# Attention rounds on one Trainium2 core: hop transposes first, score products accumulated on top

## Chip, core and metric

The kernel runs on one core of a Trainium2 chip. The metric is the device time of one execution in microseconds (us), as the median of several runs. Times inside an execution come from a hardware profile of one run.

## What is computed

The reference takes `x` and a context, each 32 batches of 512 positions by 512 features, and a 512 by 512 table of indices into 2017 rows of `rpe`. It runs an mLSTM-like cross attention with 8 heads of 64 features and then a small routed feed-forward layer. What matters here is the attention:

```python
qh = layernorm(x) split into heads;  kh, vh = context split into heads
pe = rpe[hops].reshape(S, S, NH, DH)
k_hop = einsum('bhvc,vmhc->bhvm', qh, pe)
qk = einsum('bhsd,bhtd->bhst', qh, kh / sqrt(DH))
C = (qk + k_hop) * D
h = (C / (normalizer + EPS)) @ vh
```

`D` is a causal decay, zero for keys after the query. So each weight is the sum of a score product (`qk`) and a hop product (`k_hop`), times a decay.

## The kernel before

The program has two parts. In the first, up to about 1350 us, GpSimd gathers rows of `rpe`, TensorE turns them and multiplies them with the queries of all batches, and the hop products go to DRAM. The second part, in which the change lies, works through the 32 batches as overlapping rounds: while batch b is in its attention (`ra` in the code), the next one is prepared (`rp`, `rn`) and the one before goes through its feed-forward layer (`rf`, `rg`). Every engine has its own list of steps, written out by hand in `run`, and semaphores tie the lists together.

A batch has 4 head pairs of 3 units: 12 units, in 6 double steps (`for d in range(DOUBLES)`). A unit takes two heads (`e` = 0, 1) and the causal blocks of 128 by 128 positions that `BLOCKS` lists for it: 4, 4 and 2 blocks for the three units of a pair. Two banks of PSUM belong to each unit of a double step, one bank per head. In a double step TensorE does, in this order:

- `scores` for both units (S, L1689): products of 64 features. Head 0 lies on partitions 0 to 63 and head 1 on 64 to 127, so each matmul uses half of the array's rows, and the two heads' matmuls run side by side. This shape reads `64*128` in the profile. S opens the bank (`start=(n == 0)`).
- `hop_scores` for both units (H, L1701): hop products, laid out by query, are transposed with the identity on the whole array (`128*128`) and added to what S left. Its last transpose tells VectorE that the unit is ready.
- other work on the whole array (called X below): transposes of context, queries and results (L1627), the feed-forward layer's products (L1772, L1776, L1753), a small transpose (L1737). Which of it falls into which double step is written out in the loop.
- `weigh` for both units (V, L1724): decayed weights times values, 64 output features per head, the two heads side by side on the array's columns (`128*64`). It waits for VectorE.

Two small pieces stand between V and S: the gate products (L1664, `128*32`) after the V of d = 2, and the gate rows' transposes (L1674, `40*128`) ahead of d = 5.

VectorE multiplies each ready unit by its decay (L1347). SyncE loads the hop products of a pair into `hop_in` with 16 DMAs (L667). It may do so once a unit of the pair before last has told that it is ready, and the first transposes of a pair (`k == 0`) wait until all 16 have landed. An fp32 matmul stands as two instructions in the trace, a transpose as one.

Of the kernel before, what the change touches and what calls it, by code (L numbers as in the profile page):

```python
# [5 lines left out]
P = 128  # L6
# [91 lines left out]
def build(nc, x, ctxt, hops, igate_w, igate_b, fgate_w, fgate_b, rpe, ln_w, ln_b,  # L98
# [35 lines left out]
    UNITS = len(BLOCKS) * (NH // HPT)  # L134
# [15 lines left out]
    with ExitStack() as ctx:  # L150
        def sem(name):
            return ctx.enter_context(nc.semaphore(name))

        psum = ctx.enter_context(nc.psum_tensor("psum", [P, 8 * BANK], F32))
# [4 lines left out]
        def place(n):  # L159

            top[0] += n
            assert top[0] <= ARENA, top[0]
            return arena[:, top[0] - n:top[0]]

        def bank(n, width=BANK):
            return psum[:, n * BANK:n * BANK + width]


        ident = place(P)
# [47 lines left out]
        qT = [place(KT * S).rearrange("p (k s) -> p k s", k=KT) for _ in range(2)]  # L217
        kT = [place(KT * S).rearrange("p (k s) -> p k s", k=KT) for _ in range(2)]
# [78 lines left out]
        def whole_blocks(n):  # L297

            s, c, k = GROUP[n]
            return c + (k == FULL)  # L300
# [49 lines left out]
        def hop_width(n):  # L350
            s, c, k = GROUP[n]
            return P * s + DIAG * (c + 1)
# [31 lines left out]
        def turn_bank(step):  # L384
            return bank(TURN_BANKS[turned_number[step] % len(TURN_BANKS)])
# [46 lines left out]
        pe_a = Stage(sem("pe_a"), pe_a_steps)  # L432
        dve_a = Stage(sem("dve_a"), [("mul", u) for u in units])
# [1107 lines left out]
        def _(pe):  # L1541
# [5 lines left out]
            for n, (srcs, rows_in, cols, dst, scale, split) in enumerate(jobs):  # L1547
# [10 lines left out]
                for i, src in enumerate(srcs):  # L1558
                    last = nc.tensor.transpose(bank(n % 8)[:, i * cols:(i + 1) * cols], src,
                                               ident[0:rows_in, 0:rows_in])  # L1560
# [20 lines left out]
            for n in range(GROUPS):  # L1581
                s, c, k = GROUP[n]
                width = hop_width(n)
                qt = q_turned[n % 2].rearrange("p (k v b) -> p k v b", k=KT, v=VG)
                for o in hop_order(n):
                    if o[0] in ("diag", "pack"):

                        i = o[1] % 2
                        j = o[2] if o[0] == "diag" else whole_blocks(o[1])
# [7 lines left out]
                    if o[0] != "prod":  # L1597
                        copied(bank_before(o))
                        for q in range(KT):
                            last = nc.tensor.transpose(turn_bank(o)[:, q * P:(q + 1) * P],  # L1600
                                                       own[:, q * P:(q + 1) * P], ident)
                    else:
# [9 lines left out]
                        for p in range(KT):  # L1612
                            for e in range(HPT):
                                at = (3 + 2 * (v % 2) + e) * BANK
                                half = slice(e * DH, (e + 1) * DH)
                                last = nc.tensor.matmul(  # L1616
                                    psum[p * B:(p + 1) * B, at:at + width],
                                    qt[half, p, v, :], rowsT[c % 2][half, v, p, 0:width], start=True, stop=True)
# [5 lines left out]
            def run(rn, rp, ra, rf, rg):  # L1624
# [5 lines left out]
                def turn_context(t):  # L1630

                    if t == 0:
                        pe.wait_ge(ctx_loaded, rp.b * 16 + 16)
                        if rf:
                            pe.wait_ge(dve_o.sem, dve_o.done(rf.b, ("sum", 2)))
                    elif t == 1:
                        if rg:
                            pe.wait_ge(*act_f.at(rg.b, ("mixT", ST - 1)))
                    elif t == 2:
                        if rf:  # L1640
                            pe.wait_ge(dve_o.sem, dve_o.done(rf.b, ("sum", 3)))
                    else:
                        pe.wait_ge(act_p.sem, act_p.done(rp.b, ("c", 1)))
                    turn(C_BANK[t], context[:, t, :]).then_inc(pe_p.sem, pe_p.step(("c", t)))
# [23 lines left out]
                def gate_stats():  # L1668
                    pe.wait_ge(dve_p.sem, dve_p.done(rp.b, "a"))
                    pe.wait_ge(act_p.sem, act_p.done(rp.b, "floor"))  # L1670
                    if rf:
                        pe.wait_ge(*dve_f.at(rf.b, ("out", 1)))
                    for k in range(KT):
                        last = nc.tensor.transpose(bank(6)[:, k * P:k * P + GR], g_rows[0:GR, k * P:(k + 1) * P],  # L1674
                                                   ident[0:GR, 0:GR])
                    last.then_inc(pe_p.sem, pe_p.step("stats"))

                def scores(u):


                    p, k = u // 3, u % 3
                    pe.wait_ge(dve_a.sem, dve_a.done(ra.b, ("mul", (u - 2) % UNITS), 1 if u < 2 else 0))
                    if u == 0:
                        pe.wait_ge(act_p.sem, act_p.done(ra.b, ("x", ST - 1)))
                    at = [((u % 2) * 2 + e) * BANK for e in range(HPT)]
                    for n, (j, col, width) in enumerate(RUNS[k]):
                        for e in range(HPT):
                            half = slice(e * DH, (e + 1) * DH)
                            nc.tensor.matmul(psum[:, at[e] + col:at[e] + col + width],  # L1689
                                             kT[ra.par][half, p, j * P:(j + 1) * P],  # L1690
                                             qT[ra.par][half, p, j * P:j * P + width],
                                             start=(n == 0), stop=False, skip_group_check=True)

                def hop_scores(u):
                    p, k = u // 3, u % 3
                    at = [((u % 2) * 2 + e) * BANK for e in range(HPT)]
                    if k == 0:
                        pe.wait_ge(hop_loaded[p % 2], (ra.b * 2 + p // 2 + 1) * (16 * ST * QUARTERS))
                    for n, (j, i) in enumerate(BLOCKS[k]):
                        for e in range(HPT):  # L1700
                            last = nc.tensor.matmul(psum[:, at[e] + n * P:at[e] + (n + 1) * P],  # L1701
                                                    hop_in[p % 2][:, e, Q_OFF[i] + j * P:Q_OFF[i] + (j + 1) * P],
                                                    ident, is_transpose=True, start=False, stop=True,
                                                    skip_group_check=True)
                    last.then_inc(pe_a.sem, pe_a.step(("score", u)))

                def weigh(u):

# [22 lines left out]
                def turn_back(r, p):  # L1731
                    pe.wait_ge(act_o.sem, act_o.done(r.b, ("turned", p)))
                    turn(pair_bank(p), attT).then_inc(pe_o.sem, pe_o.step(("back", p)))
# [16 lines left out]
                def routes(r, t):  # L1750
                    pe.wait_ge(*act_f.at(r.b, ("xT", t)))
                    for k in range(KT):
                        last = nc.tensor.matmul(bank(7)[:, 0:ER + E_ALL], ffn_xT[t % 2][:, k, :],  # L1753
                                                route_wT[:, k, :], start=(k == 0), stop=(k == KT - 1))
                    last.then_inc(*pe_f.inc(("route", t)))
# [22 lines left out]
                for d in range(DOUBLES):  # L1778
                    if rp and d == 5:
                        gate_stats()  # L1780
                    if ra:
                        scores(2 * d)
                        scores(2 * d + 1)
                        hop_scores(2 * d)
                        hop_scores(2 * d + 1)
                    if d == 0:
                        if rf:
                            turn_back(rf, 3)
                        if rp:
                            turn_context(0)  # L1790
                        if rg:
                            base(rg, 3)
                        elif rp:
                            turn_context(1)
                    if rp and d == 1:
                        turn_context(3)
                        turn_context(2)
                        turn_queries(0)
                        turn_queries(1)
                    if rp and d == 2:  # L1800
                        turn_queries(2)
                    if rf and d == 2:
                        turn_ffn(rf, 0)
                    if ra and d in BACK:
                        turn_back(ra, BACK[d])
                    if rp and d == 2:
                        turn_queries(3)
                    if rf and d >= 3:
                        base(rf, d - 3)
                    if rf and d >= 2:  # L1810
                        routes(rf, d - 2)
                    if ra:
                        weigh(2 * d)
                        weigh(2 * d + 1)
                    if rp and d == 2:
                        gates()

            batch_loop(pe, run)


# [25 lines left out]
```

## Time and profile before

| | us |
|---|---|
| median of 3 runs | 3316.13 |
| lowest and highest run | 3313.09, 3317.16 |
| the profiled execution | 3310.51 |
| its span, first to last instruction | 3308.5 |
| TensorE matmul busy in the span | 2938.0 |
| VectorE busy | 2417.6 |
| GpSimd busy | 2023.2 |
| ScalarE busy | 1941.4 |

The profile's engine names are PE (TensorE matmuls), PEld (TensorE weight loads), DVE (VectorE), ACT (ScalarE), POOL (GpSimd), and SP or SPq (SyncE and its DMA queue). The whole span mixes the two parts of the program, so a share of the span says little about the rounds; the rows below come from stretches within them.

### The profile page before, as it was taken

To read this page: it belongs to the slowest core of one execution; us is meant where nothing else is said; L and a number is where in the kernel's file an instruction comes from. 1 tells how busy PE (TensorE), PEld (TensorE's weight loads), DVE (VectorE), ACT (ScalarE), POOL (GpSimd) and SP (SyncE) were. 2 spreads that over 40 slices of the span, in tenths; PEclk is the share of its full clock that TensorE was granted. 3 is DMA by queue.
4 is the path that set the end of the run, shared out by engine and by line. 5 is a ranking of instruction groups with operands and counts; after the bars stand their busy time and mean duration, and the time that the engine had idled before them with its cause. 6 is when DMAs were issued, how large, how long until landed. Compare 5 with 4: busy or idle time off the path is not lost.

```text
span 3308.5 us, 69970 instructions
## 1 busy us (share of the span) xinstructions
PE 2938.0 (89%) x24660; PEld 1856.5 (56%) x24660; DVE 2417.6 (73%) x5103; ACT 1941.4 (59%) x4654; POOL 2023.2 (61%) x2195
## 2 busy tenths in 40 slices
PE   6777777777777777699999999999999999999998
PEld 4555454544544554366666666666666666666664
DVE  5655555555555555588888888888888888888875
ACT  3444444444444444477666676666766767667663
POOL 6777777777777777256455455564554645546554
PEclk8888899999999999799999999999999999999999
DMA  9999999999999999556556565565565655656542
GB/s 283 345 349 349 320 348 344 344 352 352 347 345 346 351 348 326 190 184 189 180 174 185 178 189 179 177 187 181 177 190 169 195 173 179 187 179 180 185 148 66
DMA packets 414909, 799.98 MB, mean 242 GB/s; under 512 B 107338, under 2 KB 213834, under 8 KB 412516
## 3 DMA queue, kind: packets, MB, share of 16 engines
q1 hardware_dynamic: 312516, 453.08, 43.6%
q0 software_dynamic: 82560, 270.60, 24.5%
q10 hardware_dynamic: 19488, 71.84, 5.6%
q8 instruction: 200, 3.28, 0.4%
q14 instruction: 145, 1.19, 0.1%
HBM read 618.02 MB, written 176.69 MB: 240 GB/s over the span
## 4 chain that ended last, share of the span: by engine, by line
PE 65%; DMA 16%; POOL 9%; issue 5%; DVE 4%; ACT 1%; SPq 0%; POOLq 0%; DVEq 0%; ACTq 0%
DMA arena<-in_L_xattn_rpe_dram,arena 15%; PE psum L1772 13%; PE psum L1689 9%; PE psum L1701 9%; PE psum L1724 9%; PE psum L1627 7%; PE psum L1600 6%; POOL arena L797 6%; PE psum L1616 4%; PE psum L1753 3%; PE psum L1776 3%; PE psum L1664 2%; POOL arena L782 2%; PE psum L1569 1%; DVE arena L1237 1%
## 5 line engine op out<-in xcount | busy, mean ns | idle before, releaser
L797 POOL DMA_INDIRECT arena<-in_L_xattn_rpe_dram,arena x768 | 731.8, 953 | 235.0 <-issue 181.6
L1600 PE MATMUL psum<-arena 128*128 128x128 f32 x4128 | 614.4, 297 | 190.3 <-DMA arena<-in_L_xattn_rpe_dram,arena 178.6
L1600 PEld LDWEIGHTS psum<-arena 128*128 128x128 f32 x4128 | 488.9, 151 | 422.9 <-DMA arena<-in_L_xattn_rpe_dram,arena 292.9
L993 ACT ACTIVATE arena<-arena 128x512 f32<-128x512 f32 (+3 forms) x1024 | 496.3, 555 | 43.7 <-PE psum L1724 39.2
L1772 PE MATMUL psum<-arena 128*128 128x512 f32 x1024 | 493.3, 595 | 0.0
L1347 DVE TENSOR_TENSOR arena<-psum,arena 128x1024 f32<-128x1024 f32 (+1 forms) x384 | 386.6, 1041 | 133.3 <-PE psum L1701 122.4
L573 DVE COPY arena<-psum 128x512 f32<-128x512 f32 x384 | 263.4, 689 | 239.3 <-PE psum L1600 235.5
L582 DVE COPY arena<-psum 128x416 f32<-128x416 f32 (+15 forms) x512 | 225.3, 442 | 278.4 <-PE psum L1616 270.1
L823 POOL TENSOR_SCALAR_AFFINE_SELECT arena<-arena 128x256 f32<-128x256 f32 x256 | 118.7, 464 | 503.9 <-ACT arena L993 491.6
L1616 PE MATMUL psum<-arena 64*32 64x416 f32 (+7 forms) x8192 | 361.5, 422 | 59.3 <-ACT arena L909 38.1
L573 ACT COPY arena<-psum 128x512 f32<-128x512 f32 x384 | 225.8, 588 | 251.7 <-PE psum L1600 248.7
L582 ACT COPY arena<-psum 128x416 f32<-128x416 f32 (+15 forms) x512 | 199.7, 390 | 262.9 <-PE psum L1616 255.5
L1689 PE MATMUL psum<-arena 64*128 64x512 f32 (+3 forms) x2048 | 333.1, 450 | 0.0
L1724 PE MATMUL psum<-arena 128*64 128x512 f32 (+3 forms) x2048 | 318.9, 442 | 5.1 <-ACT arena L965 2.6
L1701 PE MATMUL psum<-arena 128*128 128x128 f32 x2560 | 321.8, 277 | 0.0
L1701 PEld LDWEIGHTS psum<-arena 128*128 128x128 f32 x2560 | 276.2, 140 | 77.5 <-issue 69.9
L782 POOL DMA_INDIRECT arena<-in_L_xattn_rpe_dram,arena x264 | 250.9, 950 | 93.1 <-issue 61.8
L1627 PE MATMUL psum<-arena 128*128 128x128 f32 x2048 | 281.4, 276 | 24.2 <-DMA arena<-in_ctx_dram 11.5
L1627 PEld LDWEIGHTS psum<-arena 128*128 128x128 f32 x2048 | 237.5, 141 | 101.7 <-ACT arena L1044 39.6
L1689 PEld LDWEIGHTS psum<-arena 64*128 64x128 f32 x2048 | 181.3, 187 | 136.9 <-issue 106.5
L1772 PEld LDWEIGHTS psum<-arena 128*128 128x128 f32 x1024 | 168.1, 192 | 113.4 <-issue 113.2
L841 POOL TENSOR_TENSOR arena<-arena 128x512 f32<-128x512 f32 x128 | 159.1, 1243 | 104.4 <-ACT arena L1021 104.4
(112 smaller groups left out, 4632.1 us busy)
## 6 DMA issues: line engine op xcount, KB each, us to landing
arena<-in_x_dram SPq DMA_DIRECT2D x256, 256.0 KB, 4.1
arena<-gate_rows SPq DMA_DIRECT2D x128, 512.0 KB, 4.4
arena<-in_x_dram SPq DMA_DIRECT2D x512, 64.0 KB
arena<-in_ctx_dram SPq DMA_DIRECT2D x32, 1024.0 KB, 7.5
out_dram<-arena SPq DMA_DIRECT2D x128, 256.0 KB, 2.9
arena<-in_L_xattn_rpe_dram,arena POOLq DMA_INDIRECT x1032, 7.1
arena<-hop_products SPq DMA_DIRECT2D x128, 128.0 KB, 2.6
arena<-hop_products SPq DMA_DIRECT2D x128, 120.0 KB, 2.5
```

Source lines behind the costliest of these rows:

```text
L573: copy(rowsT[c % 2][:, o[2], :, o[3] * P:(o[3] + 1) * P], turn_bank(o).rearrange("p (k m) -> p k m", k=KT)).then_inc(*line.inc(o))
L582: copy(hop_out[out_of(n)][:, lo:lo + width], bank(3 + 2 * (v % 2) + i, width)).then_inc(*line.inc(o))
L797: nc.gpsimd.indirect_dma_start(out=rows[set_of(n, v)][:, t, :], out_offset=None, in_=rpe[:, :], in_offset=bass.IndirectOffsetOnAxis(ap=her ...
L993: last = nc.scalar.activation(decay[u % DECAYS][:, e, at:at + width], top_pair[p % 2][:, e * S + j * P:e * S + j * P + width], ACT.Exp, bi ...
L1347: nc.vector.tensor_tensor(d, got[:, :, 0:width], d, ALU.mult).then_inc(dve_a.sem, dve_a.step(("mul", u)))
L1600: last = nc.tensor.transpose(turn_bank(o)[:, q * P:(q + 1) * P], own[:, q * P:(q + 1) * P], ident)
L1616: last = nc.tensor.matmul(psum[p * B:(p + 1) * B, at:at + width], qt[half, p, v, :], rowsT[c % 2][half, v, p, 0:width], start=True, stop=True)
L1627: last = nc.tensor.transpose(bank(b)[:, k * P:(k + 1) * P], src[:, k * P:(k + 1) * P], ident)
L1689: nc.tensor.matmul(psum[:, at[e] + col:at[e] + col + width], kT[ra.par][half, p, j * P:(j + 1) * P], qT[ra.par][half, p, j * P:j * P + width],
L1701: last = nc.tensor.matmul(psum[:, at[e] + n * P:at[e] + (n + 1) * P], hop_in[p % 2][:, e, Q_OFF[i] + j * P:Q_OFF[i] + (j + 1) * P], ident, ...
L1724: last = nc.tensor.matmul(psum[e * DH:(e + 1) * DH, pair_bank(p) * BANK + j * P:pair_bank(p) * BANK + j * P + width], values[ra.par][:, j, ...
L1772: nc.tensor.matmul(bank(6), ffn_xT[t % 2][:, k, :], base_wT[:, k, :], start=(k == 0), stop=False)
```

## The change

Within each double step the calls of `hop_scores` come ahead of those of `scores`. The transposes now open the bank (`start=(n == 0)`), the score products are added to them (`start=False`), and the last score product, not the last transpose, tells VectorE that the unit is ready. The wait for VectorE to have emptied the unit's banks moves to `hop_scores`.

```diff
 def scores(u):
     p, k = u // 3, u % 3
-    pe.wait_ge(dve_a.sem, dve_a.done(ra.b, ("mul", (u - 2) % UNITS), 1 if u < 2 else 0))
     if u == 0:
         pe.wait_ge(act_p.sem, act_p.done(ra.b, ("x", ST - 1)))
...
-                nc.tensor.matmul(psum[:, at[e] + col:at[e] + col + width],
-                                 kT[ra.par][half, p, j * P:(j + 1) * P],
-                                 qT[ra.par][half, p, j * P:j * P + width],
-                                 start=(n == 0), stop=False, skip_group_check=True)
+                last = nc.tensor.matmul(psum[:, at[e] + col:at[e] + col + width],
+                                        kT[ra.par][half, p, j * P:(j + 1) * P],
+                                        qT[ra.par][half, p, j * P:j * P + width],
+                                        start=False, stop=True, skip_group_check=True)
+    last.then_inc(pe_a.sem, pe_a.step(("score", u)))

 def hop_scores(u):
...
+    pe.wait_ge(dve_a.sem, dve_a.done(ra.b, ("mul", (u - 2) % UNITS), 1 if u < 2 else 0))
     if k == 0:
         pe.wait_ge(hop_loaded[p % 2], (ra.b * 2 + p // 2 + 1) * (16 * ST * QUARTERS))
...
-                                    ident, is_transpose=True, start=False, stop=True,
+                                    ident, is_transpose=True, start=(n == 0), stop=False,
                                     skip_group_check=True)
-    last.then_inc(pe_a.sem, pe_a.step(("score", u)))
...
         if ra:
+            hop_scores(2 * d)
+            hop_scores(2 * d + 1)
             scores(2 * d)
             scores(2 * d + 1)
-            hop_scores(2 * d)
-            hop_scores(2 * d + 1)
```

In the changed kernel S is L1688 and H is L1702. Only TensorE's list differs. The double step d = 1 of a batch in mid-loop on TensorE, before (the last row is the V that follows):

```order
L1689 MATMUL psum<-arena 128x256 x2
L1689 MATMUL psum<-arena 128x512 x2
L1701 MATMUL psum<-arena 128x128 x12
L1627 MATMUL psum<-arena 128x128 x16
L1724 MATMUL psum<-arena 64x256 x2
```

The same step in the changed kernel, from the V of the step before:

```order
L1724 MATMUL psum<-arena 64x128 x2
L1702 MATMUL psum<-arena 128x128 x12
L1688 MATMUL psum<-arena 128x256 x2
L1688 MATMUL psum<-arena 128x512 x2
L1627 MATMUL psum<-arena 128x128 x16
L1724 MATMUL psum<-arena 64x256 x2
```

H and X stood side by side before, both on the whole array; now S, on half rows, stands between them. The double step d = 5, before, with the gate rows' transposes L1674 ahead of it:

```order
L1724 MATMUL psum<-arena 64x512 x2
L1674 MATMUL psum<-arena 128x40 x4
L1689 MATMUL psum<-arena 128x384 x2
L1689 MATMUL psum<-arena 128x128 x2
L1689 MATMUL psum<-arena 128x256 x2
L1701 MATMUL psum<-arena 128x128 x12
L1627 MATMUL psum<-arena 128x128 x4
```

And in the changed kernel:

```order
L1724 MATMUL psum<-arena 64x512 x2
L1674 MATMUL psum<-arena 128x40 x4
L1702 MATMUL psum<-arena 128x128 x12
L1688 MATMUL psum<-arena 128x384 x2
L1688 MATMUL psum<-arena 128x128 x2
L1688 MATMUL psum<-arena 128x256 x2
L1627 MATMUL psum<-arena 128x128 x4
```

Here S no longer follows the gate rows' transposes: H stands between them.

## Rows read from the trace of the kernel before

**Rows 1.** Busy time by stretch: the rounds in mid-loop, and one batch.
```profile
core 0: us, PE busy (x) PEld busy (x) DVE busy (x) ACT busy (x) POOL busy (x), PEclk, DMA share, GB/s
1480.00:3200.00 1720.00, 1717.46 (x10569) 1069.28 (x10568) 1496.26 (x3185) 1188.71 (x2898) 935.50 (x1038) 1.00 0.58 180
2004.72:2064.60 59.88, 59.85 (x370) 37.25 (x369) 52.25 (x112) 41.46 (x102) 32.50 (x36) 1.00 0.59 181
```

**Rows 2.** Same view, a stretch in which the first batches enter the rounds.
```profile
1364.84:1424.72 59.88, 49.82 (x364) 32.26 (x364) 41.34 (x67) 41.57 (x93) 17.70 (x31) 0.99 0.64 195
```

**Rows 3.** Chain that ended last, one batch: start us, us, what, pieces end to end.
```profile
2004.79 1.45 PE psum L1724 x12
2006.24 1.93 PE psum L1689 x12
2008.16 1.90 PE psum L1701 x16
2010.06 0.87 PE psum L1627 x8
...
2014.92 0.86 PE psum L1776 x2
2015.78 1.88 PE psum L1724 x12
2017.65 1.49 PE psum L1689 x8
2019.14 1.46 PE psum L1701 x12
2020.60 1.85 PE psum L1627 x16
2022.45 1.44 PE psum L1724 x8
2023.89 1.50 PE psum L1689 x12
2025.39 1.46 PE psum L1701 x12
...
2033.13 1.93 PE psum L1689 x12
...
2046.55 1.46 PE psum L1701 x12
2048.01 1.72 PE psum L1772 x4
...
2055.24 0.31 PE psum L1674 x3
2055.55 1.44 PE psum L1689 x12
2056.98 1.46 PE psum L1701 x12
2058.44 0.44 PE psum L1627 x4
...
2064.67 1.45 PE psum L1724 x12
```

**Rows 4.** Groups by line and shape, 1500 to 3100 us: weight loads, mean ns second.
```profile
L1701 PEld LDWEIGHTS psum<-arena 128*128 128x128 f32 x2132 | 229.9, 140 | 64.9 <-issue 58.5
L1689 PEld LDWEIGHTS psum<-arena 64*128 64x128 f32 x1704 | 149.8, 186 | 112.6 <-issue 87.6
L1772 PEld LDWEIGHTS psum<-arena 128*128 128x128 f32 x858 | 140.0, 191 | 95.0 <-issue 95.0
```

**Rows 5.** Instructions in order of time, d = 1: TensorE and VectorE.
```profile
2017.58 0.73 PEld L1689 LDWEIGHTS psum<-arena 64*128 64x128 f32 x8 [0.17 <-issue]
2017.58 1.56 PE L1689 MATMUL psum<-arena 64*128 64x256 f32 x8
...
2019.77 0.69 DVE L1347 TENSOR_TENSOR arena<-psum,arena 128x512 f32<-128x512 f32 x1 [1.73 <-PE psum L1701]
...
2020.33 1.88 PEld L1627 LDWEIGHTS psum<-arena 128*128 128x128 f32 x16
2020.44 2.01 PE L1627 MATMUL psum<-arena 128*128 128x128 f32 x16
```

**Rows 6.** The same view for SyncE's queue: the loads of hop products, pairs 1 and 2.
```profile
2005.30 8.54 SPq L667 DMA_DIRECT2D arena<-hop_products  x16
...
2019.76 8.62 SPq L667 DMA_DIRECT2D arena<-hop_products  x16
```

**Rows 7.** Line L667, 1500 to 3100 us: issue to landing.
```profile
DMA to landing us min/median/max: 1.5/2.1/4.3
```

## Prediction

> **What bounds the kernel now.** I first read the busy time by stretch. In the rounds TensorE's matmuls cover 1717.46 of 1720 us, with the granted clock at 1.00, which is the 2.4 GHz level, while VectorE has 1496.26 [rows 1]. One batch in mid-loop shows 59.85 of 59.88 us; from one V of d = 5 at 2004.79 to the next at 2064.67 [rows 3] it is 59.88 us too. A busy share alone could hide waits, so I then read the chain that ended last over one batch: it consists of TensorE pieces that follow each other without a gap [rows 3]. In the rounds, therefore, time is what TensorE's own list takes, and the pieces of that list are the thing to cost. The first part of the program, before about 1350 us, is not touched.
>
> **What a piece costs beyond its columns.** In the chain the reader should compare each piece with what its matmuls would take in a steady stream. Eight transposes that follow others of the same layout take 0.87 us, so one takes 0.109 us; a matmul of 512 columns takes 0.43 us (L1776, two in 0.86) [rows 3]. Against that:
>
> - H after S: 16 transposes are 1.74 us and took 1.90; 12 are 1.31 and took 1.46. Entering costs 0.155 us.
> - S after V: of the 12 instructions at 2006.24 six pairs run side by side, 2048 columns, 1.72 us; they took 1.93. The 8 at 2017.65 are 1536 columns, 1.29 us, and took 1.49. Entering costs 0.20 to 0.21 us.
> - V after X: 1536 columns, 1.29 us, took 1.45 and 1.44; 2048 columns, 1.72, took 1.88. Entering costs 0.16 us.
> - X after H: the 8 transposes at 2010.06 are the steady stream itself, so entering costs nothing; H and X have one layout, the whole array [rows 3].
>
> So TensorE pays 0.15 to 0.21 us each time the layout changes (whole array, half rows, half columns), and nothing otherwise. It is not the semaphore waits: H in d = 2 has no wait for hop data, H in d = 1 has one, and both took 1.46 us [rows 3]. It is not the adding onto a filled bank either: V opens its bank in d = 0 and adds in d = 1, and pays 0.16 and 0.15 us.
>
> **The change, part by part.** No matmul, weight load or transpose is added, and the other engines' lists stay. What changes is the number of layout changes. Before, a double step runs V | S | H and X | V: three entries. After, it runs V | H | S | X | V: four, since S now separates H from X.
>
> - Ordinary steps (d = 0 to 3; X begins with transposes): out go S after V (0.21) and H after S (0.155), in come H after V, S after H and X after S. No row shows H after V or S after H. The known entries lie between 0.15 and 0.21 us, and the cost follows what is entered: I take 0.155 for whole-array transposes and 0.21 for S, because these rows are those of the same arriving instructions. X after S arrives with the same kind of transpose as H does: 0.155. Net 0.155 + 0.21 + 0.155 - 0.21 - 0.155 = +0.155 us. In d = 3 the gate products stand between V and S, and the exchange is the same.
> - d = 4: X begins with L1772, whose weight load takes 191 ns, like that of S (186) and unlike that of a transpose (140) [rows 4]. So its entry is put at 0.21 and the step at +0.21 us.
> - d = 5: the gate rows' transposes L1674 use 40 rows, and S after them took 1.44 us for 1.29, an entry of 0.15 [rows 3]. Now H (0.155), S (0.21) and X (0.155) are entered, where S (0.15) and H (0.155) were: +0.21 us.
>
> Per batch 4 x 0.155 + 0.21 + 0.21 = 1.04 us; times 32, 33.3 us. In the stretch where the first batches enter, TensorE is busy for only 49.82 of 59.88 us [rows 2], so there, and likewise at the end, part of it fits into waits; I count 30.5 batches: **+31.7 us**. Against the profiled execution's 3310.5 us this gives 3342; its time stands 5.6 us below the median of 3316.13, so the forecast on the median is **3348 us**.
>
> The bounds: with every new entry at the cheapest one seen (0.15), the steps give 4 x 0.09 + 0.09 + 0.15 = 0.60 us, 18 us in all, 3334. With every new entry at the dearest (0.21), they give 5 x 0.265 + 0.325 = 1.65 us, 50 us in all, 3366.
>
> What rests on cover: VectorE's start. The first unit of d = 1 was handed over 2.19 us after the step began (2017.58 to 2019.77) [rows 5]: S 1.49, H's entry 0.155, four transposes 0.44. Now it is H 1.46, S's entry 0.21, 256 columns in two passes 0.43: 2.10. The second unit is ready at the end of H and S in either order. So VectorE gets its data at about the same distance from V, and X, the cover of its multiplication, even ends 0.155 us later. I cost this at nothing. The moved wait on VectorE is past already: the V ahead of it waited for the same multiplications. The freeing of `hop_in` shifts as little, since it hangs on the same signal.
>
> **A rule beside the rows.** When S begins at 2017.58, its first weight load begins at 2017.58 too, after 0.17 us of idle time, whereas the load for X at 2020.33 runs ahead of its matmul at 2020.44 [rows 5]. The Trainium skill (TensorE: Matmul & The Clock Gate, Part 2, on loading the stationary operand) says that TensorE pulls weight loads ahead of running matmuls. If that held across layout changes too, an entry would shrink by the length of the load and this change would cost some 0.02 us a step, about 3320 us as an estimate; the rows agree with it within a layout and not across one, so I go by the rows. Another page, TensorEngine Tiling (Array Packing), Key Properties, says that changing the tiling mode drains the engine, and lists 128x128, 128x64 and 64x128 as modes of their own: that covers H after V as well, which no row here shows, and speaks against this change.
>
> **Rivals.**
>
> - *Leaving V is free* (3324 us). If whole-array transposes after half columns cost no entry, an ordinary step stays as it was (0.21 + 0.155 either way), d = 4 gains 0.055 and d = 5 keeps 0.21: 0.265 x 30.5 = 8 us more. For it: no row shows this entry. Against it: the opposite change, X to V, costs 0.16 [rows 3].
> - *Faster: the 0.155 at H is a wait for S's results in the bank* (3289 us). Then H, which now opens the bank, has nothing to wait for, and X after S pays nothing either. An ordinary step and d = 4 would lose 0.155 us, d = 5 0.095: 0.87 x 30.5 = 26.5 us less. It decides if H after V and X after S cost under half of 0.155. Against it: V pays the same whether it opens or adds, and S, which opened its banks, paid most.
> - *Hop data come late* (about 3380 us). H now needs its data earlier: pair 1 some 0.6 us into d = 1 instead of 2.1, pair 2 at the start of d = 3. The issues for pair 1 end at 2013.84; with the median landing time of 2.1 us the data are there at 2015.9, with the longest of 4.3 at 2018.1, and H of that pair is due at 2018.2 [rows 5 to 7]. Pair 2's issues end at 2028.38, so its data arrive between 2030.5 and 2032.7, and S of d = 3 began at 2033.13 [rows 3, 6, 7]. So there are 2.3 and 2.6 us to spare at the median and next to nothing at the longest. If landings came 3.3 us later than the median, one such wait of 1 us per batch would add 32 us. Against it: the step begins later too, by what the entries add.
>
> **How the numbers follow.** Forecast 0.83, hop data late 0.08, leaving V free 0.05, faster 0.04. The range 3334 to 3366 takes in the bounds of the entries; outside it lie the rivals, 0.17. A measurement of this kernel can tell about 0.2% from no change, 6.6 us, so 3309.5 to 3322.7 counts as the same. The rival at 3324 lies on that line; I give 0.03 of it to the same and 0.02 to slower. Slower is then 0.83 + 0.08 + 0.02 = 0.93, same 0.03, faster 0.04.
>
> **What would show it right or wrong.** Right: a batch in mid-loop takes about 60.9 us instead of 59.88, TensorE stays busy throughout at a granted clock of 1.00, H at L1702 still takes 1.90 and 1.46 us, S at L1688 1.93 and 1.49, and the first piece of X after S takes 0.15 us more than its columns (8 transposes of d = 0: 1.03 us instead of 0.87). Wrong: H after V without the 0.155, X after S at 0.87 us, or idle time of TensorE ahead of L1702 ended by the hop loads.

## The result, and the profile after

| | us |
|---|---|
| forecast (range) | 3348 (3334 to 3366) |
| median of 3 runs after | 3342.20 (3341.34 to 3347.30) |
| median of 3 runs before | 3316.13 |
| the profiled execution after | 3341.34 |
| its span, first to last instruction | 3339.3 |

The changed kernel is slower: the ratio to the kernel before is 1.0086, with a 95% interval of 1.0073 to 1.0100, and the medians differ by 26.1 us. The two profiled spans differ by 30.8 us. Time in the rounds is still what TensorE's list takes. Busy time of the changed kernel in mid-loop (columns as in [rows 1]):

```profile
1480.00:3200.00 1720.00, 1718.09 (x10414) 1047.68 (x10416) 1461.16 (x3128) 1172.39 (x2856) 907.88 (x1019) 1.00 0.58 178
```

1718.09 of 1720 us are covered by matmuls and the granted clock is 1.00, as in [rows 1]; in the same stretch of time TensorE got through 10414 matmul instructions instead of 10569. So it is not idle more, it needs longer. Where the time went can be read piece by piece in the chain that ended last (start us, us, what), from V of d = 4 of one batch to V of d = 5 of the next:

```profile
2003.16 1.44 PE psum L1724 x8
2004.60 0.37 PE psum L1674 x4
2004.97 1.46 PE psum L1702 x12
2006.43 1.50 PE psum L1688 x12
2007.93 0.58 PE psum L1627 x4
...
2014.31 1.45 PE psum L1724 x12
2015.76 1.90 PE psum L1702 x16
2017.65 1.93 PE psum L1688 x12
2019.58 1.02 PE psum L1627 x8
...
2027.32 1.46 PE psum L1702 x12
2028.78 1.49 PE psum L1688 x8
2030.28 2.00 PE psum L1627 x16
...
2056.59 1.49 PE psum L1688 x8
2058.09 1.92 PE psum L1772 x4
...
2075.22 1.45 PE psum L1724 x12
```

The reader should hold these against [rows 3]. H (now L1702) takes 1.90 and 1.46 us, as before, although it now follows V. S (now L1688) takes 1.93 and 1.49, as before, although it now follows H. What grew is the first piece of X, which now follows S: 8 transposes 1.02 instead of 0.87, 16 transposes 2.00 instead of 1.85, the first feed-forward products 1.92 instead of 1.72, 4 transposes 0.58 instead of 0.44. From one V of d = 5 to the next it is 75.22 - 14.31 = 60.91 us, against 59.88 before: 1.03 us more per batch.

The boundaries themselves, in order of time, in d = 1 of the changed kernel:

```profile
2027.25 1.29 PEld L1702 LDWEIGHTS psum<-arena 128*128 128x128 f32 x12 [0.17 <-issue]
2027.25 1.53 PE L1702 MATMUL psum<-arena 128*128 128x128 f32 x12
2028.71 0.73 PEld L1688 LDWEIGHTS psum<-arena 64*128 64x128 f32 x8 [0.17 <-issue]
2028.71 1.56 PE L1688 MATMUL psum<-arena 64*128 64x256 f32 x8
2029.46 0.69 DVE L1347 TENSOR_TENSOR arena<-psum,arena 128x512 f32<-128x512 f32 x1 [1.75 <-PE psum L1688]
2030.20 0.42 PEld L1627 LDWEIGHTS psum<-arena 128*128 128x128 f32 x4 [0.76 <-issue]
2030.21 0.55 PE L1627 MATMUL psum<-arena 128*128 128x128 f32 x3
```

At each of the three new boundaries the first weight load starts with its stretch and not ahead of it, after idle time of the loader (`[0.17 <-issue]`, `[0.76 <-issue]`): for X at 2030.20 too, whose loads ran 0.11 us ahead of the matmuls in [rows 5], where X followed H. VectorE starts 2.21 us after the step began (2027.25 to 2029.46), against 2.19 before.

### The profile page after: what moved, and what is told of

The parts are those of the page before. It is cut to its first block, busy times and chain, and to the rows that moved or that the text cites. A ratio compares the mean times of both kernels' runs of the same rounds, so it can differ in the third digit from the quotient of the medians.

```text
span 3339.3 us, 70066 instructions
## 1 busy us (share of the span) xinstructions
PE 2979.8 (89%) x24660; PEld 1858.7 (56%) x24660; DVE 2408.2 (72%) x5103; ACT 1942.2 (58%) x4654; POOL 2011.5 (60%) x2195
## 4 chain that ended last, share of the span: by engine, by line
PE 69%; DMA 15%; POOL 7%; issue 4%; DVE 3%; ACT 1%; SPq 1%; DVEq 0%; POOLq 0%; ACTq 0%
DMA arena<-in_L_xattn_rpe_dram,arena 14%; PE psum L1772 13%; PE psum L1688 9%; PE psum L1702 9%; PE psum L1724 9%; PE psum L1600 7%; PE psum L1627 7%; POOL arena L797 6%; PE psum L1616 4%; PE psum L1753 4%; PE psum L1776 3%; PE psum L1664 2%; POOL arena L782 1%; PE psum L1569 1%; DVE arena L1237 1%
## 5 line engine op out<-in xcount | busy, mean ns | idle before, releaser
L1600 PE MATMUL psum<-arena 128*128 128x128 f32 x4128 | 623.4, 300 | 180.8 <-DMA arena<-in_L_xattn_rpe_dram,arena 167.1
L1772 PE MATMUL psum<-arena 128*128 128x512 f32 x1024 | 495.4, 597 | 0.0
L1688 PE MATMUL psum<-arena 64*128 64x512 f32 (+3 forms) x2048 | 328.7, 449 | 0.0
L1702 PE MATMUL psum<-arena 128*128 128x128 f32 x2560 | 324.2, 278 | 1.7 <-DMA arena<-hop_products 1.7
L1702 PEld LDWEIGHTS psum<-arena 128*128 128x128 f32 x2560 | 278.4, 141 | 79.5 <-issue 78.0
L1627 PE MATMUL psum<-arena 128*128 128x128 f32 x2048 | 289.6, 280 | 23.4 <-DMA arena<-in_ctx_dram 11.4
L1772 PEld LDWEIGHTS psum<-arena 128*128 128x128 f32 x1024 | 167.6, 191 | 136.6 <-issue 129.6
L1688 PEld LDWEIGHTS psum<-arena 64*128 64x128 f32 x2048 | 171.1, 186 | 99.1 <-issue 63.0
```

Source lines behind the costliest of these rows:

```text
L1627: last = nc.tensor.transpose(bank(b)[:, k * P:(k + 1) * P], src[:, k * P:(k + 1) * P], ident)
L1688: last = nc.tensor.matmul(psum[:, at[e] + col:at[e] + col + width], kT[ra.par][half, p, j * P:(j + 1) * P], qT[ra.par][half, p, j * P:j * ...
L1772: nc.tensor.matmul(bank(6), ffn_xT[t % 2][:, k, :], base_wT[:, k, :], start=(k == 0), stop=False)
```

## Experiments

The theory: each entry into another layout costs TensorE 0.15 to 0.21 us, by what is entered, and the change adds one entry per double step. The rivals that could give the same slowdown: that H first or S last costs something by itself, or that H meets its data too early. Times of a batch below are the distance of the same V in two successive batches. The edits are shown shortened: the calls of a double step stand on one line, and lines that only follow from what is shown are left out.

**More entries, H still after S.** The units interleaved in the order of before:

```diff
-scores(2 * d); scores(2 * d + 1); hop_scores(2 * d); hop_scores(2 * d + 1)
+scores(2 * d); hop_scores(2 * d); scores(2 * d + 1); hop_scores(2 * d + 1)
```

> The kernel before with the two units' calls interleaved: S of the first unit, H of the first, S of the second, H of the second, then X. Nothing is added but two changes of layout per double step (S after H, H after S). Theory (each entry into another layout costs what the entered instructions cost, 0.155 us for transposes and 0.20 to 0.21 for S): +0.36 us per double step, 6 x 0.36 = 2.2 us per batch, a batch of 62.05 us, and with 30 batches some +65 us, near 3381. Rival (the cost lies in H coming first and S last, not in the number of entries): H still follows S and X still follows H here, so no change, near 3316. Rival (H waits for S's results in the bank): here H follows S of its own unit at once, so each H would wait longest, with H pieces beyond 0.155 us over their stream.

Measured: 3372.19 us against 3314.18, a ratio of 1.0176 (1.0156 to 1.0195), 58 us more. Chain that ended last in this kernel, the pieces of a d = 4 step and, first and last, V of d = 1 in two batches:

```profile
2041.82 1.44 PE psum L1724 x8
...
2065.07 0.63 PE psum L1689 x4
2065.71 0.59 PE psum L1701 x4
2066.30 1.06 PE psum L1689 x4
2067.35 1.02 PE psum L1701 x8
2068.38 1.72 PE psum L1772 x4
...
2103.75 1.44 PE psum L1724 x8
```

S takes 0.63 us for 512 columns (0.43) and 1.06 for 1024 (0.86): 0.20 at each entry. H takes 0.59 for 4 transposes (0.44) and 1.02 for 8 (0.87): 0.15. X after H, which begins with L1772, pays nothing (1.72). A batch takes 61.93 us, 2.05 more where 2.17 was expected. So order is not what costs: H follows S and X follows H here as in the kernel before. H right behind S of its own unit pays no more than elsewhere.

**Six entries.** The changed kernel, interleaved:

```diff
-hop_scores(2 * d); hop_scores(2 * d + 1); scores(2 * d); scores(2 * d + 1)
+hop_scores(2 * d); scores(2 * d); hop_scores(2 * d + 1); scores(2 * d + 1)
```

> The changed kernel with the two units interleaved: H of the first unit, S of the first, H of the second, S of the second, then X. Six entries per double step where the kernel before has three and the changed one four. Theory: H after V 0.16, S after H 0.20, H after S 0.16, S after H 0.20, X after S 0.16, against S after V 0.21 and H after S 0.16: +0.51 us in d = 0 to 3, some +0.56 in d = 4 and 5, 3.2 us per batch, a batch of 63.06 us, some +95 us, near 3411. Rival (only the place of H and S against V and X counts): as the changed kernel, a batch of 60.91 us, near 3342.

Measured: 3403.97 us, a ratio of 1.0271 (1.0252 to 1.0291), 90 us more. V of d = 0 in two batches, from the chain:

```profile
2046.37 1.87 PE psum L1724 x12
...
2109.38 1.88 PE psum L1724 x12
```

63.01 us per batch, 3.13 more than before; 3.2 was expected. With three, four, five and six entries per double step a batch takes 59.88, 60.91, 61.93 and 63.01 us: each entry adds 1.02 to 1.08 us per batch, 0.17 to 0.18 us per double step.

**Four entries, X after H.**

```diff
-scores(2 * d); scores(2 * d + 1); hop_scores(2 * d); hop_scores(2 * d + 1)
+hop_scores(2 * d, True); scores(2 * d, False); scores(2 * d + 1, True); hop_scores(2 * d + 1, False)
```

The second argument says who opens the unit's banks: in the first unit H, in the second S.

> H of the first unit opens its banks, S of both units follows, H of the second unit comes last and adds, then X. Four entries per double step, as in the changed kernel, but X follows H as before, H adds in one unit as before, and the second unit's hop data are needed as late as before. Theory: entries 0.16 + 0.20 + 0.16 against 0.21 + 0.16, +0.155 us per double step, 0.21 in d = 5: a batch of 60.87 us (0.04 less than in the changed kernel, whose d = 4 pays 0.20 for entering the feed-forward products after S), some +29 us, near 3345. Rival (the cost of the change is that X no longer follows H): back to the kernel before, near 3316. Rival (hop data needed earlier): most of the cost gone, since units 3 and 9 need theirs as late as before.

Measured: 3338.86 us, a ratio of 1.0074 (1.0055 to 1.0093), 24.7 us more. In this kernel V is L1730, S L1690, H L1706; chain that ended last, d = 0, and V of d = 3 in two batches:

```profile
2053.03 1.88 PE psum L1730 x12
...
2076.39 1.02 PE psum L1706 x8
2077.41 1.93 PE psum L1690 x12
2079.34 1.02 PE psum L1706 x8
2080.36 0.87 PE psum L1627 x8
...
2113.88 1.87 PE psum L1730 x12
```

X is back at 0.87 us behind H, and the 0.15 that it lost stands in the second H instead (1.02 for 0.87). A batch takes 60.85 us, 0.06 less than in the changed kernel; 60.87 was expected. Neither the place of X nor the time at which hop data are needed explains the cost; the number of entries does.

**The changed kernel again**, beside these three:

> The changed kernel once more, beside the others on one chip: 3342, between 3336 and 3350, a batch of 60.91 us.

Measured: 3344.24 us (3338.31 to 3349.42) against 3314.18, a ratio of 1.0094 (1.0073 to 1.0114).

**The hop data, needed early.** Only the wait is moved, from `hop_scores` to ahead of the double step's S:

```diff
-if k == 0:
-    pe.wait_ge(hop_loaded[p % 2], (ra.b * 2 + p // 2 + 1) * (16 * ST * QUARTERS))
...
+for u in (2 * d, 2 * d + 1):
+    p = u // 3
+    if u % 3 == 0:
+        pe.wait_ge(hop_loaded[p % 2], (ra.b * 2 + p // 2 + 1) * (16 * ST * QUARTERS))
 scores(2 * d)
```

> The kernel before with one thing moved: TensorE waits for the pair's hop data ahead of S of the double step, not ahead of H. This is the earlier need for data that the change brings, without its new entries. Theory (the data have landed by then): no change, 3316 within 0.2%, a batch of 59.88 us, no idle time of TensorE ended by the loads. Rival (hop data come late): each batch waits at d = 1 or d = 3, every 1 us of it 32 us in the run, and the changed kernel's +26 us would be this.

Measured: 3315.17 us against 3313.98, a ratio of 1.0007 (0.9998 to 1.0016): no change that can be told. Waits of its matmuls in the rounds (1360 to 3300 us) on the hop loads, and, second, those of the changed kernel: us in total, times, longest:

```profile
PE psum L1689 <- DMA arena<-hop_products: 1.8, 3, 1.1
...
PE psum L1702 <- DMA arena<-hop_products: 1.7, 1, 1.7
```

Three waits in 32 batches, 1.8 us in all, and one of 1.7 us in the changed kernel.

The data are there in nearly every batch.

**Who opens the bank.** The kernel before, with one flag changed in `hop_scores`:

```diff
-    ident, is_transpose=True, start=False, stop=True,
+    ident, is_transpose=True, start=(n == 0), stop=True,
```

> The kernel before with the transposes opening the banks anew instead of adding: order, waits, shapes and columns as before. What it leaves out: the score products, which the transposes overwrite. Theory (the entry cost belongs to the layout, not to adding): no change, 3316 within 0.2%, H at 1.90 and 1.46 us. Rival (the 0.155 us at H is a wait for S's results in the bank): 0.155 x 6 x 30 = 28 us less, near 3288, H at 1.74 and 1.31 us.

Measured: 3314.74 us against 3313.98, a ratio of 0.9999 (0.9990 to 1.0008). From its chain, H of d = 0 and of d = 1:

```profile
2069.35 1.90 PE psum L1701 x16
...
2080.33 1.46 PE psum L1701 x12
```

The same 1.90 and 1.46 us as with adding. The entry cost does not belong to adding onto S. H still follows S into the same bank here, so this run alone does not rule out a wait for S; the changed kernel does, where H follows V into banks emptied before and takes the same time.

**Fewer entries.** If an entry is the price, taking some away should give time back. V of d = 0 needs nothing that would keep it from running together with V of d = 1:

```diff
-DECAYS = 4
+DECAYS = 6
+WEIGHED = {1: (0, 1, 2, 3), 2: (4, 5), 4: (6, 7, 8, 9), 5: (10, 11)}
...
-weigh(2 * d)
-weigh(2 * d + 1)
+for u in WEIGHED.get(d, ()):
+    weigh(u)
```

> The kernel before with V of d = 0 done together with V of d = 1, and V of d = 3 with V of d = 4 (6 decay buffers instead of 4, so that no decay waits for it). Nothing is added or left out; two entries per batch are gone: X is then followed by S, which is entered at 0.20 where it was 0.21 after V, and V after X (0.15) is saved twice. Theory: 0.3 us less per batch, a batch of 59.58 us, with 30 batches 9 us less, near 3306, 0.997 of before. Rival (the cost of the change is its order, not its entries): the order of S and H is that of before, so no gain, 1.000. Rival (TensorE is not alone on the path): VectorE's multiplications or the decays show as idle time of TensorE ahead of S in d = 1 and 4, and the gain is eaten.

> The same joining of V in the changed kernel. There X of d = 0 and d = 3 is then followed by H, which has the same layout and needs no entry: V after X (0.15) and H after V (0.16) are both saved, twice per batch. Theory: 0.62 us less per batch than the changed kernel, a batch of 60.29 us, some 18 us less than the changed kernel, near 3325, 1.003 of before. Rival (H first costs by itself): only V after X is saved, 0.3 us per batch, near 3334, 1.006 of before.

Measured: 3330.86 us for the first, a ratio of 1.0052 (1.0040 to 1.0065) to the kernel before, and 3352.77 for the second, 1.0111 (1.0094 to 1.0127). Both are slower than the kernels they were made from: a miss. Waits of the first in 1500 to 3100 us, the longest line of TensorE's matmuls:

```profile
PE psum L1665 <- DVE arena L1355: 23.2, 26, 0.9
```

and, in order of time, one of them:

```profile
2097.84 1.27 POOL L847 TENSOR_TENSOR arena<-arena 128x512 f32<-128x512 f32 x1
2097.91 1.23 DVE L1303 TENSOR_SCALAR arena<-arena 128x8 f32<-128x8 f32 x1
...
2098.69 0.61 ACT L1015 ACTIVATE arena<-psum 128x504 f32<-128x504 f32 x1
...
2100.19 0.67 DVE L1355 TENSOR_REDUCE arena<-psum 128x8 f32<-128x504 f32 x1
...
2101.01 1.92 PE L1665 MATMUL psum<-arena 128*32 128x512 f32 x16 [0.89 <-DVE arena L1355]
```

The gate products behind d = 2 (L1665 here) wait for VectorE's sums of pair 0 (L1355), and TensorE stands for 0.89 us in every batch. A batch takes 60.47 us, from 2061.25 to 2121.72 in its chain, and 60.47 - 0.89 = 59.58 is what the theory gave for it without this wait. The second kernel waits there too (`PE psum L1665 <- DVE arena L1355: 19.4, 27, 0.7`), and a batch takes 61.08 us where 60.29 was expected. In the kernel before, this spot was covered by a hair. In order of time there:

```profile
2028.18 1.27 POOL L836 TENSOR_TENSOR arena<-arena 128x512 f32<-128x512 f32 x1
...
2028.91 0.57 DVE L1302 TENSOR_SCALAR arena<-arena 128x8 f32<-128x8 f32 x1
...
2029.72 0.61 ACT L1014 ACTIVATE arena<-psum 128x504 f32<-128x504 f32 x1
...
2030.39 0.67 DVE L1354 TENSOR_REDUCE arena<-psum 128x8 f32<-128x504 f32 x1
...
2031.21 1.93 PE L1664 MATMUL psum<-arena 128*32 128x512 f32 x16
```

VectorE's sums ended at 2031.06, 0.15 us before the gate products began.

The expectation of the next run holds that the sums were late because the V of d = 1 now comes behind the V of d = 0. The rows do not bear that out. ScalarE's squares, through which the sums wait for that V (L1014 before, L1015 here), ended 6.4 us after S of d = 2 began in both kernels (S at 2023.89 and 2092.90), and here they had been done for 0.9 us when the sums began. The sums began 7.29 us after that S, where it had been 6.50, because VectorE was still at two short steps ahead of them in its list (L1302 before, L1303 here): they took 1.23 and 0.52 us instead of 0.57 and 0.38, 0.80 us more in all. The same kind of step took 0.17 us at 2092.78, when GpSimd did nothing beside it. The long ones began during a GpSimd instruction and ended 0.03 us after it (2099.14 after L847 at 2099.11; before, 2029.48 after L836 at 2029.45). The joining moved VectorE's step to the start of such an instruction, where it had met the latter half of one. Why the two end together was not tested.

**Only the later joining.** So d = 0 to 2 were left as they were:

```diff
-WEIGHED = {1: (0, 1, 2, 3), 2: (4, 5), 4: (6, 7, 8, 9), 5: (10, 11)}
+WEIGHED = {0: (0, 1), 1: (2, 3), 2: (4, 5), 4: (6, 7, 8, 9), 5: (10, 11)}
```

> The kernel before with only V of d = 3 done together with V of d = 4 (6 decay buffers); d = 0 to 2 as before. One entry per batch is gone. Theory: 0.15 us less per batch, a batch of 59.73 us, some 4.5 us less, near 3309, 0.9986 of before; that the joining of d = 0 and 1 lost time comes from the gate products behind d = 2, which wait for VectorE's sums of pair 0 and so for V of d = 1. Rival (any joining delays VectorE): a batch above 59.88 us, with TensorE waiting in d = 4 or 5.

> The same joining in the changed kernel: X of d = 3 is followed by H of the same layout, so V after X (0.15) and H after V (0.16) are both saved once per batch. Theory: 0.31 us less per batch than the changed kernel, a batch of 60.60 us, some 9 us less, near 3333, 1.006 of before. Rival (H first costs by itself, whatever it follows): only V after X is saved, a batch of 60.76 us, near 3338.

Measured: in the order of before 3312.15 us against 3313.99, a ratio of 0.9994 (0.9985 to 1.0004), which does not tell a gain from none; in the changed order 3334.63 us, a ratio of 1.0061 (1.0047 to 1.0075). The joined V in two successive batches, in order of time, of the first:

```profile
2235.04 3.23 PE L1725 MATMUL psum<-arena 128*64 128x512 f32 x20
...
2294.73 3.23 PE L1725 MATMUL psum<-arena 128*64 128x512 f32 x20
```

and of the second, whose later rows show two batches without a wait for the gate rows:

```profile
2305.36 3.23 PE L1725 MATMUL psum<-arena 128*64 128x512 f32 x20
...
2365.97 3.23 PE L1725 MATMUL psum<-arena 128*64 128x512 f32 x20
```

59.69 us per batch (59.73 expected, 59.88 before), and 60.61 (60.60 expected, 60.91 without the joining). In the second, H follows X of its own layout and its entry is gone as well: 0.30 us for one joining, where the rival allowed 0.15. Some batches of both wait up to 0.8 us for ScalarE's gate rows at L1675 (five in 1500 to 3100 us of the first), so the 0.19 us per batch of the first do not all arrive in the total. The gate products behind d = 2 have no wait on the sums in that stretch of either, so it is the joining of d = 0 and 1 that brought it. No version was found that is shown to beat the kernel before.

## Why the prediction was right

- *TensorE's list is the bound.* Shown: it is covered to 1718.09 of 1720 us after, at the same clock.
- *One entry more per double step, priced by what is entered.* Shown row by row: H after V costs what H after S cost, S after H what S after V cost, and X after S 0.15 us. The forecast for d = 4, 0.21 because of the longer weight load of L1772, measured 0.20 (1.92 for 1.72).
- *d = 5.* S now takes 1.50 us where it took 1.44, H 1.46 as before, X 0.58 where it took 0.44, and the gate rows' transposes 0.37 for 0.31: +0.26 us by the chain's pieces, forecast +0.21. The prediction misread a row here: it took S behind the gate rows' transposes for an entry of 0.15. In the kernel before, S begins there before the last of these transposes does:

```profile
2055.32 0.59 PE L1689 MATMUL psum<-arena 64*128 64x384 f32 x1
2055.38 0.23 PE L1674 MATMUL psum<-arena 40*128 40x40 f32 x1
```

That transpose ends at 2055.61, 0.37 us after V as in the changed kernel, and S ends at 2056.98, 1.37 us later where its columns take 1.29: 0.08 for this entry. With 0.08 in place of 0.15 the prediction's sum for d = 5 is +0.28, against the 0.26 measured.

- *Sum.* 1.04 us per batch forecast, 1.03 measured; that the two agree so closely is in part luck. From the start of one V to the next, the steps d = 0 to 5 grew by 0.15, 0.16, 0.08, 0.17, 0.20 and 0.27 us in the chains; forecast were 0.155 four times and 0.21 twice. What d = 5 took more than forecast, d = 2 took less: X ends there with L1753, which took 1.02 us before and 0.98 after, 0.94 in other steps, so part of the new entry seems to have gone into a wait that had been there; that was not tested. The factor of 30.5 batches, an estimate that no run tests by itself, gave 31.7 us; the spans of the profiled runs differ by 30.8, the medians by 26.1 and, in the second measurement, 30.1. Single runs of either kernel spread over several us, so that last step is as exact as the measurement.
- *Cover.* VectorE got its data at the same distance (2.21 us after the step began, before 2.19; the forecast of 2.10 added up TensorE's pieces only, which gives 2.09 for the kernel before). TensorE's matmuls waited for VectorE's multiplications 4 times in all the rounds, 2.3 us, against 4 times and 2.6 us before. The hop data were there.
- *The rivals.* Leaving V free fell by the H pieces of 1.90 and 1.46 us behind V. The wait for S's results in the bank fell by the same pieces, since H there follows V, and by X behind S, which writes other banks and paid 0.15; the flag experiment agrees. Late hop data fell by the moved wait.
- *The two rules.* That TensorE pulls weight loads ahead (the Trainium skill, TensorE: Matmul & The Clock Gate, Part 2) holds within a layout and not at the three boundaries shown in order of time above; the sum by it, 3320 us, lies below every run of the changed kernel. That a change of tiling mode drains the engine (the Trainium skill, TensorEngine Tiling (Array Packing), Key Properties) agrees with the traces for H after V too, where it had stood without a row: 12 transposes took 1.46 us for 1.31.

What the entry consists of is not settled beyond that: the rows show the loader idle, then load and matmul starting together, but no row separates emptying the array from loading it.

## What to carry to other kernels

Where TensorE's list is the whole path, count the changes of its tile layout (whole array, half rows, half columns) in a period and price each by the row of the instructions that are entered; a reordering that adds none of TensorE's work still costs if it separates two stretches of one layout. Before taking an entry away, look for the spot that is covered by a hair: the joining of two V stretches saved its 0.30 us per batch and lost 0.89 to a wait one double step later, which 0.15 us had kept hidden. The cause of such a wait need not be the one that the order of the steps suggests: here it stood between two other engines.

## What the runs showed beyond that

Among whole array, half rows and half columns the entry price does not depend on the layout that is left: whole-array transposes cost 0.15 to 0.16 us behind half columns and behind half rows alike, and S cost 0.20 to 0.21 behind V and behind H. The exception is S behind the gate rows' transposes of 40 rows, at 0.08: there the loads and matmuls of the two interleave, while H behind the same transposes pays its 0.15. So not every change of shape is an entry; what sets the two cases apart was not tested. And a transpose takes 0.109 us in a stream whether it opens a bank or adds to one.
